# A two-layer network on one core: band attention's first projections inside the experts' last batch, VectorE's factors in PSUM, and the feed-forward layer's norms inside the attention's last unit

## What is computed

```python
h = _layernorm(x) * (1 + ca) + sa
x = x + ga * L0_attn(h)      # ln1, then softmax attention (16 heads of 8, causal) and a selective
                             # state-space scan (16 states) beside each other, ln2, GELU FFN 128-512-128
h = _layernorm(x) * (1 + cb) + sb
x = x + gb * L0_ffn(h)       # routed experts: 8 of 128-512-128 with SiLU, plus a shared one, top 2
h = _layernorm(x) * (1 + ca) + sa
x = x + ga * L1_attn(h)      # band attention across the batch axis: 65 keys of which 8 exist
h = _layernorm(x) * (1 + cb) + sb
x = x + gb * L1_ffn(h)       # token shift, r = sigmoid(..), k = relu(..)**2, r * (k @ W)
```

## Time and profile before

| | |
|---|---|
| median of 3 runs | 1677.8 us (1675.17 to 1679.55) |
| the profiled execution's own time | 1669.76 us |
| its span in the trace | 1668.0 us |
| busy share of the span: TensorE | 84% |
| VectorE | 76% |
| ScalarE | 66% |
| GpSimd | 52% |
| mean granted clock of TensorE | 0.934 of full |

### The profile page before, as it was taken

One profiled execution on the slowest core, in us unless ns is written; L12 is line 12 of the kernel. 1 busy time (PEld: TensorE's weight loads), 2 busy tenths in 40 slices (PEclk: granted clock), 3 DMA queues, 4 the chain that ended last, 5 costly groups with the idle time before them and its releaser, 6 DMA issues. The chain is left out here.

```text
span 1668.0 us, 22123 instructions
## 1 busy us (share of the span) xinstructions
PE 1408.5 (84%) x7164; PEld 884.0 (53%) x7164; DVE 1261.6 (76%) x1873; ACT 1093.5 (66%) x1864; POOL 863.4 (52%) x889
## 2 busy tenths in 40 slices
PE   3688898888989898887767887999999999868687
PEld 3234444444444444444324645787786877725573
DVE  2149999989798988989915858687686767848857
ACT  2475668686767778786746736777878788621017
POOL 3137677778696978878843113022222222248843
PEclk9787899999999999999988989999999999979889
DMA  3112222222222222222003010111111111000001
GB/s 90 45 39 83 77 63 78 80 75 70 64 68 67 78 73 68 80 76 75 27 1 95 19 48 26 33 48 45 40 49 39 45 45 45 26 0 1 0 1 50
DMA packets 61688, 84.73 MB, mean 51 GB/s; under 512 B 6621, under 2 KB 32071, under 8 KB 61575
## 3 DMA queue, kind: packets, MB, share of 16 engines
q1 hardware_dynamic: 61474, 83.30, 16.0%
q10 hardware_dynamic: 100, 0.03, 0.0%
HBM read 74.38 MB, written 8.78 MB: 50 GB/s over the span
## 5 line engine op out<-in xcount | busy, mean ns | idle before, releaser
L1760 POOL TENSOR_TENSOR dBx<-dtx,Bb 128x512 f32<-128x512 f32 x256 | 319.6, 1272 | 11.4 <-DMA Bb<-b_dram 10.1
L1355 DVE TENSOR_TENSOR hl<-lsq,hh 128x512 fp32r<-128x512 f32 x320 | 259.5, 821 | 86.7 <-ACT hh L1644 78.9
L1325 DVE TENSOR_TENSOR_SCAN hy<-bank,dBx 128x512 f32<-128x512 f32 x256 | 297.8, 1203 | 10.5 <-ACT bank L1628 6.0
L1641 ACT ACTIVATE lsq<-bank,vcol 128x512 f32<-128x512 f32 x320 | 219.4, 692 | 108.1 <-DVE hl L1355 61.0
L1050 PE MATMUL bank<-QK 127*128 127x128 bf16 (+7 forms) x1024 | 237.7, 318 | 46.6 <-DVE Mx L1315 27.9
L1315 DVE TENSOR_REDUCE Mx<-bank 128x1 f32<-128x384 f32 (+3 forms) x352 | 212.1, 627 | 57.5 <-PE bank L1050 56.7
L1784 POOL TENSOR_TENSOR stage<-stage,lrs 128x512 f32<-128x512 f32 x64 | 92.3, 1443 | 310.5 <-DVE lrs L1435 310.5
L1050 PE MATMUL bank<-x,we1h 128*128 128x512 f32 x640 | 210.7, 411 | 18.8 <-DVE x L1343 9.4
L1569 ACT ACTIVATE PT<-bank 128x512 f32<-128x512 f32 x320 | 183.7, 596 | 52.9 <-PE bank L1050 51.3
L1628 ACT ACTIVATE bank<-dtv,alog 128x512 f32<-128x512 f32 x256 | 170.4, 692 | 61.2 <-DVE hy L1325 60.8
L1050 PEld LDWEIGHTS bank<-QK 127*128 127x128 bf16 (+1 forms) x1024 | 94.3, 104 | 191.9 <-issue 51.5
(11 more groups left out here) (258 smaller groups left out, 2393.6 us busy)
## 6 DMA issues: line engine op xcount, KB each, us to landing
Bb<-b_dram SPq DMA_DIRECT2D x128, 256.0 KB, 3.6
stage<-w_rows SPq DMA_DIRECT2D x64, 256.0 KB, 3.2
parts<-part SPq DMA_DIRECT2D x16, 384.0 KB, 2.7
QK<-parts SPq DMA_DIRECT2D x64, 96.0 KB
QK<-parts SPq DMA_DIRECT2D x64, 64.0 KB
stage<-in_L_ffn_We_dram SPq DMA_DIRECT2D x16, 256.0 KB, 3.3
hy<-in_L_attn_x_dram SPq DMA_DIRECT2D x8, 256.0 KB, 5.8
QK<-parts SPq DMA_DIRECT2D x64, 32.0 KB
```

Of the source, the lines that this page charges most:

```text
L1325: engine.tensor_tensor_scan(hst[:, 2 * (g % 3) + h, :], bank[4 + h][:], dBx[:, g % 4, h, :], 0.0, ALU.mult, ALU.add).then_inc(sems["dve_sc ...
L1355: engine.tensor_tensor(hl[:, sl, :], full[:, f, :], hh[:, sl, :].bitcast(F32), ALU.subtract).then_inc(sems["dve_hl"], 1)
L1641: engine.activation(full[:, f, :], o[:], fn, bias=bias).then_inc(sems["act_up"], 1)
L1760: engine.tensor_tensor(dBx[:, sl, h], dtx[:, b % 2, h], Bb[:, sl], ALU.mult).then_inc(sems["pool_dbx"], 1)
```

## The change

Five edits, three at the border between mixers and FFN and two in the band attention.

1. `second_norms` puts the norms ln2 of batches 0 to 5 between the score tiles of unit 15, that of batch 6 between the first two and last two chunks of the FFN's batch 0, and that of batch 7 inside the FFN's batch 4 (`LAST_NORM`). They use the tile `part` for squares.
2. `plan_ffn` becomes a generator: the FFN's weights and first input are loaded and split once the scan is done, and its batches start right behind the step `on` of the last attention group. The weights of e = 8, 0, 1, 2 are split inside batches 2 to 5. Up steps take banks from the ring, down steps banks 4 and 5. For this the memory is laid out anew, so that the FFN's tiles lie over the scan's (one tile `wall` for all weights), and batch 7's scan has no `beside` pieces, since the tile that they use holds the first norm's results.
3. The chunk c = 2 is cast by VectorE in the FFN too.
4. The constants and the eight projections of group 0 move from the band attention into the experts: the constants ahead of batch 0, one projection ahead of each expert of batch 7.
5. VectorE takes four of the eight score products (`Q_DVE`), and its factors lie in PSUM: ScalarE copies these q into bank 5, 3 or 2, and the softmax writes the weights of s = 1, 4, 7 a second time, into bank 7 (`weights4`, one small multiplication per group more). Projections of groups 1 to 3 take turns on two banks instead of four; values use banks 4 to 6.

```diff
         it["o"] = free["Os"] = free[f"lrs{hf}"] = on = up("pool_on")
+        if (b, g) == (NB - 1, 3):
+            ends["on"] = True
...
-                      y_free=free.get("yT"), y_last=ssm[b]["y"][half], beside=b >= 2 and n in BESIDE, yb_free=free.get(f"yB{half}", nT_read))
+                      y_free=free.get("yT"), y_last=ssm[b]["y"][half], beside=2 <= b < NB - 1 and n in BESIDE, yb_free=free.get(f"yB{half}", nT_read))
...
+        ends["ssm"] = tuple(p.last.values())
...
+    def second_norms():
+        for b in range(NB):
+            while ended[b] < 2 or b == NB - 1 and ends.get("ffn", 0) < LAST_NORM:
+                yield
+            k = take()
+            ring.remove(k)
+            finish_norm = p.norm_start((k, ring[0]), (h_last[b],), kind="ln2", b=b, square="part", dst_free=(free.get("yB0"), free.get("yB1")) if b < 2 else None)
+            for _ in range(2):
+                yield
+            r_h2[b] = finish_norm()
+            ring.append(k)
+            yield
 
...
+    seconds = second_norms()
     for u in range(NU):
-        run_together(attend(u), 20, (mixer, SSM_RATE, False), (tops, 23, False), (prepare(u), 8, True))
+        last = 1 if u == NU - 1 else 0
+        run_together(attend(u), 20, (mixer, SSM_RATE, False), (tops, 23, False), (prepare(u), 8, True),
+                     (seconds, 16 * last, False), (behind_it, 20 * last, False))
+    drain(mixer)
     while late or later:
         settle(0)
-    drain(mixer)
+        next(seconds, None)
+        next(behind_it, None)
+    ends["att"] = tuple(p.last.values())
+    ring.append(3)
+    for _ in behind_it:
+        next(seconds, None)
...
+        k = p.first_free(self.ring) if self.ring else c
+        it = p.step("up", b=b, e=e, c=c, sl=sl, f=f, bank=k, ready=(self.split_done[b], self.w_done[e]), free=p.free.get(f"b{k}"),
                     lsq_free=p.free.get(f"lsq{f}"), hh_free=p.free.get(f"hh{sl}"))
         it["m"] = p.free[f"x3{b % 2}"] = p.up("pe_up")
-        it["x"] = p.free[f"b{c}"] = p.up("act_up")
-        if c == 2 and e < 9:
+        it["x"] = p.free[f"b{k}"] = p.up("act_up")
+        if c == 2:
             it["y"] = p.up("dve_hh")
         else:
-            it["y"] = p.free[f"b{c}"] = p.up("act_up")
+            it["y"] = p.free[f"b{k}"] = p.up("act_up")
         it["z"] = p.free[f"lsq{f}"] = p.up("dve_hl")
...
-ON_DVE = (1, 4, 7)
-
-
-def plan_ffn(p, x, h_last, done):
+Q_DVE = (1, 3, 5, 7)
+V_DVE = (1, 4, 7)
+
+
+def plan_ffn(p, x, r_h2, r_x2, ring, ends):
 
     free, up, step = p.free, p.up, p.step
-    r_h2, r_x2, r_xT, l_x2 = [None] * NB, [None] * NB, [None] * NB, {}
-    bk = ((0, 4), (1, 5), (2, 6), (3, 7))
-    drain(p.norms([(r_h2, b, (bk[b % 4], (h_last[b], *done)), dict(kind="ln2", b=b)) for b in range(NB)]))
-    x.split_weights(0, 9, done)
+    r_xT, l_x2, split = [None] * NB, {}, [0]
 
     def ffn_end(b, e, k, m):
         it = step("ffn_end", b=b, bank=k, m=m, ready=(r_h2[b], r_xT[b]))
@@ -578,24 +606,55 @@
         it["x"] = r_x2[b] = up("dve_fe")
 
     def load_x(b):
-        it = step("x2load", b=b, free=free.get(f"xin2{b % 2}"), done=done)
+        it = step("x2load", b=b, free=free.get(f"xin2{b % 2}"), done=ends["ssm"])
         l_x2[b] = it["d"] = up(f"x2_in{b % 2}", 16)
 
+    while "ssm" not in ends:
+        yield
+    x.split_weights(0, 9, ends["ssm"])
     load_x(0)
-    x.split(0, r_h2[0], done)
+    while not r_h2[0]:
+        yield
+    x.split(0, r_h2[0], ends["ssm"])
+    while "on" not in ends:
+        yield
     for b in range(NB):
+        ends["ffn"] = b
         if b + 1 < NB:
             load_x(b + 1)
-            x.split(b + 1, r_h2[b + 1], done)
-        if b < 4:
-            x.split_weights(b + 1, (8, 0, 1, 2)[b])
-        k = 4 + b % 2
-        it = step("x2tr", b=b, bank=k, free=free.get(f"b{k}"), ready=l_x2[b], done=done)
+            while not r_h2[b + 1]:
+                yield
+            x.split(b + 1, r_h2[b + 1], ends["ssm"])
+        if "att" in ends and split[0] < 4:
+            x.split_weights(split[0] + 1, (8, 0, 1, 2)[split[0]], ends["att"])
+            split[0] += 1
+        k = p.first_free(ring)
+        it = step("x2tr", b=b, bank=k, free=free.get(f"b{k}"), ready=l_x2[b], done=ends["ssm"])
         it["m"] = free[f"xin2{b % 2}"] = up("pe_x2")
         it["x"] = free[f"b{k}"] = r_xT[b] = up("act_x2")
-        drain(x.run(b, 9, ffn_end))
-    drain(x.run(None, None, None))
-    return r_x2
+        yield from x.run(b, 9, ffn_end)
+    yield from x.run(None, None, None)
+    for i in range(split[0], 4):
+        x.split_weights(i + 1, (8, 0, 1, 2)[i], ends["att"])
...
+def q_bank_of(r):
+    return 5 if r == 0 else 2 + r % 2
+
+
+def project4(p, r, r_h4, r_qkv, done):
+
+    free, up = p.free, p.up
+    r_qkv[r] = []
+    for s in range(8):
+        k, kq = s % 2 if r else 4, q_bank_of(r)
+        it = p.step("qkv", rg=r, s=s, bank=k, ready=(r_h4[2 * r], r_h4[2 * r + 1]), free=free.get(f"b{k}"), qkv_free=free.get(f"qkv{r % 3}"),
+                    q_free=free.get(f"b{kq}"), done=done)
+        it["m"] = up("pe_q4")
+        it["x"] = up("act_q4", 2)
+        free[f"b{k}"] = it["x"]
+        r_qkv[r].append(it["x"])
+        yield
...
+    done_shared = tuple(p.last.values())
+    step("band_const", done=done_shared)
+    up("dve_bk", 8)
...
+            if b == NB - 1:
+                if e == 0:
+                    ahead = project4(p, 0, r_h4, r_qkv, done_shared)
+                next(ahead)
             drain(x.run(b, e, moe_end))
...
-    step("band_const", done=done)
-    up("dve_bk", 8)
...
-            it["x"] = up("dve_p4") if s in ON_DVE else up("pool_p4")
+            it["x"] = up("dve_p4") if s in Q_DVE else up("pool_p4")
+            if s == Q_DVE[-1]:
+                free[f"b{q_bank_of(r)}"] = it["x"]
...
-            k = 4 + 2 * (r % 2) + s // 4
+            k = 4 + (2 * r + s // 4) % 3
...
-    drain(project4(0))
-    run_together(scores4(0), 8, (project4(1), 8, True))
+    run_together(scores4(0), 8, (project4(p, 1, r_h4, r_qkv, done), 8, True))
...
+        def q_bank(r, s):
+            i = Q_DVE.index(s)
+            return bank[q_bank_of(r)][:, P * i:P * i + P]
+
+        def weights4(r):
+            n = 64 * len(V_DVE)
+            return bank[7][:, n * (r % 2):n * (r % 2) + n].rearrange("p (k s h) -> p k s h", k=8, h=8)
 
...
-                        engine.tensor_tensor(prod[:, w], qkv[:, r % 3, 0, s:s + 1, :].broadcast_to([P, 8, P]), qkv[:, r % 3, 1],
+                        engine.tensor_tensor(prod[:, w], q_bank(r, s).rearrange("p (o c) -> p o c", o=1).broadcast_to([P, 8, P]), qkv[:, r % 3, 1],
...
+                    ws = slice(V_DVE[0], V_DVE[-1] + 1, V_DVE[1] - V_DVE[0])
+                    engine.tensor_tensor(weights4(it["rg"]), sc.rearrange("p k (s h) -> p k s h", h=8)[:, :, ws, :],
+                                         sm1[:].rearrange("p (o s h) -> p o s h", o=1, h=8)[:, :, ws, :].broadcast_to([P, 8, len(V_DVE), 8]),
+                                         ALU.mult).then_inc(sems["dve_sm4"], 1)
...
-                    pr4 = scs[:, r % 2, :, 8 * s:8 * s + 8].rearrange("p k (h o) -> p k h o", o=1).broadcast_to([P, 8, 8, 16])
+                    pr4 = weights4(r)[:, :, V_DVE.index(s), :].rearrange("p k (h o) -> p k h o", o=1).broadcast_to([P, 8, 8, 16])
...
-                    engine.activation(t[:, 0, it["s"], :], o[:, 0:128], ACT.Copy, scale=0.25).then_inc(sems["act_q4"], 1)
+                    on_dve = it["s"] in Q_DVE
+                    q.wait_ge(it["m"], it["qkv_free"], it["q_free"] if on_dve else None, it["done"])
```

138 lines of the change are left out of this document (72 added, 66 removed).

## The result

The changed kernel takes 1654.3 us (median of 4 runs, 1652.0 to 1658.2) against 1676.5 of the kernel before: ratio 0.9868, 95% interval 0.9843 to 0.9894, 18 to 26 us less. The profiled execution took 1653.39 us, its span is 1651.7.

What follows compares the result with a forecast made beforehand. It took different engines to bound each stage: VectorE the mixers, TensorE the experts, VectorE and GpSimd together the band attention. Gains of 4.2 (border) and 21.1 (band) gave 25 off 1677.8: 1653 us, own range 1646 to 1661, 80% within 1641 to 1668.

Steps and rivals of the forecast that it cites:

- Part A: Border of mixers and FFN: a net gain of 4.2 us, with ends at -5 and +11.
- part B: Band attention, including its start: a gain of 21.1 us, between 15 and 26.
- Pieces of batch 7: Mixers: 12 pieces move to VectorE, which has little idle time; 5.3 us lost (bounds 3 and 5.7).
- Six norms and queues in unit 15: Unit 15's tail: norms cost 6.8 us (4.5 to 10.3), GpSimd's subtractions waiting ahead of selects 1 (0 to 3).
- `Os,seld` to the last activation of batch 0: FFN's start: from 881.9 to 896.3 instead of 908.36, a gain of 12.0 us.
- The rest of the FFN: FFN after batch 0: 3.3 us lost to a fourth batch with splits, 3.5 to batch 7's norm (0 to 5.2).
- Rival 1: Border of mixers and FFN at its costly end, norms at 10.3: about -6 there, 1663 us in all (22%).
- Products: Band attention: VectorE's products take 1.22 us with a PSUM factor; turns 32.5, 26.5 and 26.2, scores 0 16.4.
- rivals 3 and 4: Band attention, gain 52.7 - 25x at product time x: conflict stays, 1674 (5%); slow repeated PSUM reads, 1686 (5%).
- Last values and what follows: Band attention's end: the last values are bound by TensorE and gain 0.4 us.
- Start: Band attention's start: 15.0 us gained ahead of the first product, 9.7 paid in the experts, together +5.3.
- The distance of 8 us between median and profiled execution: Whole kernel: the profiled execution lay 8.0 us below the median of runs, and this distance was kept.

Runs made afterwards that it cites:

- e2: Changed kernel with the band attention's edits undone, only the border's edits kept: 1678.2 us, ratio 1.0021 to the kernel before.
- e5: Changed kernel, but batch 7's pieces go through ScalarE and GpSimd as before: 1648.0 us, ratio 0.9842 to the kernel before.
- g3: Changed kernel with batch 7's pieces beside, FFN weight split five tiles later and one table for Ln and Exp: 1648.5 us, ratio 0.9847 to before.
- g1: Changed kernel, but casts and subtractions of the FFN's weights stand five of unit 15's tiles later: 1660.0 us, ratio 0.9918 to the kernel before.
- e6: Changed kernel, but norms ln2 of batches 0 to 5 run as a block behind the attention: 1662.7 us, ratio 0.9922 to the kernel before.
- e1: Changed kernel with the border edits undone, only the band attention's edits kept: 1650.2 us, ratio 0.9855 to the kernel before.
- f1: Changed kernel, but group 0's constants and projections stand behind the experts again, on four banks: 1662.9 us, ratio 0.9931 to the kernel before.
- f2: Kernel before, with seven unused matmuls added in TensorE's idle 5.8 us ahead of the first projection: 1666.6 us, ratio 0.9949 to the kernel before.

## Why the prediction was right or wrong

The total, 1653 against 1654.3, was right, but in part by luck: two errors of opposite sign are in it. Part A came out 7.7 us below its forecast and part B 3 above, and the kernel before was 1.3 us faster in this comparison (1676.5) than the 1677.8 that the forecast starts from.

**Part A, forecast as a gain of 4.2 us, is a loss of 2.7 in the traces and 3.5 by e2.** By its steps:
- Pieces of batch 7: 5.3 forecast, 7 in the traces, 4.4 by e5's time (not clear of noise), 8.6 in the trace of g3 against that of g1. The forecast was too small; why the traces exceed the 5.7 of bare instructions is open.
- Six norms and queues in unit 15: 6.8 + 1.0 forecast, 12.4 measured. This is the step that failed: the two terms together were taken 4.6 us too small. I had put GpSimd's subtractions at 1, bounded at 3; e6, which has no norms there, shows 4.2, of which 1.6 is a longer wait and 2.7 TensorE's clock behind it, a cost that the prediction does not have. The norms took 8.2 if that split costs the changed kernel as much, and up to 12.4 if it doesn't; either is above my 6.8, and the second above my upper bound of 10.3. Which of the two terms was off by how much stays open.
- `Os,seld` to the last activation of batch 0: 14.5 forecast, 15.5 measured (889.28 to 904.82). The rest of the FFN: 6.8 more forecast, 6.3 measured (57.2 against 50.95). Both near.

Rival 1 (A at its costly end, -6) comes closer to what happened in this part than the forecast. By e6 the norms between the tiles are still worth 9 us against a block of them behind the attention; the loss is in the sum. In the traces A pays 7.2 us for the pieces, 12.4 in unit 15 and 6.3 in the rest of the FFN, against 23.1 gained between the last `Os,seld` and the last activation of batch 0.

**Part B, forecast 21.1, is 24 by e1.**
- Products: scores 0 at 16.5 us (forecast 16.4), turns at 32.2, 26.8 and 26.8 (32.5, 26.5, 26.2). The 1.22 taken from the pieces and reductions of the earlier trace rows was right, and rivals 3 and 4 fall with it. Their formula, 52.7 - 25x, leaves out the 4.9 us of norms that stay in the first turn; with them it is about 48 - 25x, so rival 3 stood for a loss of 1 us rather than a gain of 3.5.
- Last values and what follows: 0.4 gain forecast, 1.1 loss in the trace (34.6 from the last softmax to the next norm, 33.5 before).
- Start: 14.9 gained ahead of the first product and 9.3 paid in the experts (9.7 forecast), a net of 5.6 in the profiled pair. But f1 says 10.6. The term was mis-sized since it was read from one execution, in which the projections ran at full clock from the third on; f2, f1 and the 52 executions of the kernel before show that most executions have them at half clock.

**The distance of 8 us between median and profiled execution** I carried over unchanged. It wasn't an offset of the measurement but this clock: a projection at 1.2 GHz costs 1 us more than at 2.4, the profiled execution of before escaped that from the third on, and the changed kernel, whose first projections lie between experts, can't meet it. Accordingly its median and its profiled execution are 0.9 us apart. f2's 8.5 us agree in size. Of the 8 us, the traces account for 6.2: the first product comes 21.2 us behind the end of x3 in e2 and f1, 15.0 in the profiled execution of before. The rest is open.

The traces add up: -2.7 for A, 5.6 for the start, 15.1 for scores 0 and the turns, -1.1 and -0.6 for what follows, together the 16.3 by which the spans differ.

## What to carry to other kernels

Where VectorE and GpSimd multiply side by side out of SBUF, move one operand of the VectorE instruction to PSUM: here both engines' instructions then took nearly their shortest time, and the turn came near VectorE's own sum (24 to 25 of 26.8 us). Before work is moved into another engine's gaps, ask for each queue that it passes what waits behind it there: selects that stood behind a weight split in GpSimd's queue made TensorE wait, the next tiles ran at half its clock, and shifting the split only exposed the next wait. And read a stretch behind a long TensorE gap from more than one execution; a median well above the profiled time (here 8 us) can be a sign that the trace shows the lucky case, and the mean granted clocks of the timed runs can tell.

## What the runs showed of the hardware

The granted clock behind one and the same idle stretch of 5.8 us differs between executions: back at full by the third projection in the earlier trace rows, at 0.50 for 14 us and more in f1, although TensorE is busy without a pause in both. Filling the stretch with seven unused matmuls kept the clock at 1.00 and made the old kernel 0.5% faster. Shorter waits were followed by it too: behind 3.17 us in e6 and 4.08 in g1 the next tiles ran at 0.50, for some 5 and 3 us.
